# Stationary operands of the three-pass matmuls moved to 64 bytes behind the moving ones (modulo 512 bytes)

## The reference, cut to what matters

```
h = tok(x)                       # embedding + 4 layers; layer: x += ssm(ln(x)); x += gelu(ln(x) @ w1 + b1) @ w2 + b2
h = h + attn(layernorm(h))       # 16 heads of 16, Gaussian scores exp(-gamma * dist), masked, @ Wo
h = h + ffn(layernorm(h))        # 2 layers: shifted tokens, qkv (8 heads of 64), rotary, windowed softmax, @ wo,
                                 #           then gated MLP: a * gelu(g), width 682, @ w2
ssm(x) = scan(x @ B) @ C + x @ D # h[t] = sigmoid(a) * h[t-1] + u[t]
```

## Time and profile before

| | |
|---|---|
| three runs, us | 1294.94, 1297.45, 1292.15; median 1294.94 |
| span of the profiled execution, us | 1293.8 |
| median of the runs less that span, us | 1.1 |
| busy TensorE matmul, weight load | 94%, 80% |
| busy VectorE, ScalarE, GpSimd | 76%, 67%, 48% |
| granted TensorE clock, mean | 0.987 of full |

### The profile page before, as it was taken

One profiled execution on the slowest core, in us unless ns is written; L12 is line 12 of the kernel. 1 busy time (PEld: TensorE's weight loads), 2 busy tenths in 40 slices (PEclk: granted clock), 3 DMA queues, 4 the chain that ended last, 5 costly groups with the idle time before them and its releaser, 6 DMA issues.

```text
span 1293.8 us, 26097 instructions
## 1 busy us (share of the span) xinstructions
PE 1218.6 (94%) x8899; PEld 1035.8 (80%) x8899; DVE 988.7 (76%) x2624; ACT 860.9 (67%) x1989; POOL 618.5 (48%) x678
## 2 busy tenths in 40 slices
PE   5899999999999999799978899999999999999997
PEld 4699988988898989567756567888888887888796
DVE  5766676666667776799878988888888888888743
ACT  2455765676566556589964668777777777777754
POOL 6423341351145233455434568556556657655542
PEclk9999999999999999899989999999999999999999
DMA  7400010000000000310010002000100000000000
GB/s 170 112 1 15 2 65 0 14 32 32 0 8 1 1 1 1 75 49 18 18 53 17 1 5 93 6 5 6 49 4 3 21 6 13 22 22 22 22 17 26
DMA packets 39615, 33.25 MB, mean 26 GB/s; under 512 B 16774, under 2 KB 36178, under 8 KB 39506
## 3 DMA queue, kind: packets, MB, share of 16 engines
q1 hardware_dynamic: 38610, 29.74, 7.6%
q0 software_dynamic: 768, 2.10, 0.9%
q10 hardware_dynamic: 128, 0.04, 0.0%
HBM read 25.84 MB, written 4.19 MB: 23 GB/s over the span
## 4 chain that ended last, share of the span: by engine, by line
PE 45%; DVE 6%; ACT 3%; POOL 3%; issue 3%; DVEq 0%; ACTq 0%; POOLq 0%
PE w_ps_p L1887 3%; PE w_ring L1947 3%; PE w_ring L1948 3%; PE w_ring L1949 3%; PE w_ring L1846 3%; PE w_ring L1848 3%; PE w_ring L1847 3%; PE w_ps_a L1905 2%; PE a_ps L911 2%; PE w_ring L1959 2%; PE w_ps_d L1880 2%; PE w_ps_d L1877 2%; PE w_ring L1864 2%; PE w_ring L1960 2%; PE w_ring L1963 1%
## 5 line engine op out<-in xcount | busy, mean ns | idle before, releaser
L383 ACT ACTIVATE t_gf<-t_ps_f,t_fb_cur 128x512 f32<-128x512 f32 x128 | 87.9, 687 | 170.2 <-PE t_ps_f L289 167.0
L302 PE MATMUL t_ps_o<-t_w_hi,t_g_hi 128*128 128x256 f32 x512 | 146.1, 285 | 3.2 <-DVE t_g_lo L533 3.2
L533 DVE TENSOR_TENSOR t_g_lo<-t_gf,t_g_hi 128x512 fp32r<-128x512 f32 x128 | 94.4, 739 | 71.3 <-ACT t_g_hi L385 70.4
L304 PE MATMUL t_ps_o<-t_w_hi,t_g_lo 128*128 128x256 f32 x512 | 144.8, 283 | 0.0
L303 PE MATMUL t_ps_o<-t_w_lo,t_g_hi 128*128 128x256 f32 x512 | 144.7, 283 | 0.0
L686 POOL TENSOR_TENSOR t_rs<-t_ve,t_neghalf 128x4 f32<-128x4 f32 x32 | 37.9, 1185 | 168.0 <-DVE t_ve L494 166.6
L1947 PE MATMUL w_ring<-w_nh,w_w_hi 128*128 128x256 f32 x352 | 103.8, 295 | 3.3 <-DVE X L2546 1.7
L287 PE MATMUL t_ps_f<-t_nh,t_w_hi 128*128 128x512 f32 x256 | 103.0, 402 | 1.8 <-DVE t_nl L509 0.8
L302 PEld LDWEIGHTS t_ps_o<-t_w_hi,t_g_hi 128*128 128x128 f32 x512 | 97.7, 191 | 7.8 <-issue 4.4
L2717 POOL TENSOR_TENSOR w_m<-w_m 128x512 f32<-128x512 f32 x64 | 84.2, 1316 | 37.5 <-DVE w_m L2437 37.2
L288 PE MATMUL t_ps_f<-t_nh,t_w_lo 128*128 128x512 f32 x256 | 101.3, 396 | 0.0
(11 more groups left out here) (317 smaller groups left out, 4259.5 us busy)
## 6 DMA issues: line engine op xcount, KB each, us to landing
t_raw<-in_L_tok_w SPq DMA_DIRECT2D x8, 1024.0 KB, 5.2
out<-X SPq DMA_DIRECT2D x14, 256.0 KB, 2.2
raw<-in_L_ffn_wqkv SPq DMA_DIRECT2D x2, 1536.0 KB, 6.7
raw<-in_L_ffn_w SPq DMA_DIRECT2D x4, 640.0 KB, 5.0
w_raw_o<-out SPq DMA_DIRECT2D x8, 256.0 KB, 2.7
w_xs<-X SPq DMA_DIRECT2D x14, 127.0 KB
w_raw<-in_L_ffn_w SPq DMA_DIRECT2D x2, 640.0 KB
t_raw_d<-in_L_tok_D SPq DMA_DIRECT2D x4, 256.0 KB, 2.9
```

What stands on the lines that cost most here:

```text
L302: pe.matmul(out, g_hi[:, j % 4, tok], w2_hi[:, j, :], start=(j == 0 and t % 2 == 0), stop=False, skip_group_check=True)
L304: mm = pe.matmul(out, g_lo[:, j % 4, tok], w2_hi[:, j, :], start=False, stop=(j == FC - 1 and t % 2 == 1), skip_group_check=True)
L383: act.activation(gf[:, j % 2, :], ps_f[:, j % 2, :], ACT.Gelu, bias=fb_cur[:, j:j + 1]).then_inc(pf_free, 1)
L533: dve.tensor_tensor(g_lo[:, j % 4, :], gf[:, j % 2, :], g_hi[:, j % 4, :].bitcast(F32), ALU.subtract).then_inc(g_split, 1)
```

## The change

Empty buffers (`apart1`, `apart2`) are put in, and small ones are moved, so that in every three-pass matmul the stationary operand begins 64 bytes behind the moving one modulo 512 bytes. No instruction is added, removed or moved; only addresses change.

```
 tower:
+        sb("apart1", [P, 16])
         nf = [sb(f"nf{k}", [P, DC, GTOK]) for k in (1, 2)]
-        nh = [sb(f"nh{k}", [P, DC, GTOK], F32R) for k in (1, 2)]
-        nl = [sb(f"nl{k}", [P, DC, GTOK], F32R) for k in (1, 2)]
+        nh1, nl1 = (sb(x, [P, DC, GTOK], F32R) for x in ("nh1", "nl1"))
         hs = sb("hs", [P, GTOK])
...
         g_hi = sb("g_hi", [P, 4, GTOK], F32R)
         g_lo = sb("g_lo", [P, 4, GTOK], F32R)
+        sb("apart2", [P, 96])
+        nh2, nl2 = (sb(x, [P, DC, GTOK], F32R) for x in ("nh2", "nl2"))
+        nh, nl = [nh1, nh2], [nl1, nl2]
 attention:
         xn = [sb(f"xn{k}", [P, ST, D]) for k in range(2)]
+        sb("apart1", [P, 24])
         nh = sb("nh", [P, DC, STOK], F32R)
...
         sq = [sb(f"sq{t}", [P, 2 * D]) for t in range(ST)]
+        sb("apart2", [P, 64])
         ot_hi = sb("ot_hi", [P, HO, STOK], F32R)
 window_opening:
-    x0_ve = sb("x0_ve", [P, GT])
-    x0_rs = sb("x0_rs", [P, GT])
     xs = sb("xs", [P, 2, ST, P])
     ah = sb("ah", [P, DC, STOK], F32R)
     al = sb("al", [P, DC, STOK], F32R)
+    x0_ve = sb("x0_ve", [P, GT])
+    x0_rs = sb("x0_rs", [P, GT])
 window:
         nmr = sb("nmr", [P, ST])
+        mx = sb("mx", [P, 2 * H, 2])
         xn = sb("xn", [P, ST, D])
         nh = sb("nh", [P, DC, STOK], F32R)
...
         pt = sb("pt", [P, PTS, SC])
-        mx = sb("mx", [P, 2 * H, 2])
         rsum = sb("rsum", [P, SLOTS, 2])
```

## The result

The changed kernel takes 1287.28 us (median of 6 runs, 1283.3 to 1289.59) against 1294.4 (6 runs) before: 0.9933, interval 0.9914 to 0.9951, about 7 us less. 1276 was forecast and 1263 to 1290 given as the range. The time lies in the range, and the kernel is faster as forecast (the interval reaches the 0.5% that was named as the limit of a measurement); of the 18 us two fifths came.

A forecast was written before the change was run, and what follows sets the result against it. Matmul spacing was taken to bound tower and window, with VectorE and ScalarE equally full in attention. Gains of 25.1 us less 6.9 not kept left 18.2 us, giving 1276 us, range 1263 to 1290.

The forecast's parts named there:

- The bound: How closely matmuls follow each other sets the end in tower and window; in attention VectorE and ScalarE also do.
- (c): Tower `hidden`: 768 matmuls of 512 columns from 0 to +64, 6 ns gained each, 4.6 us.
- (e): Window phase `project`: 576 matmuls of 512 columns from 0 to +64, 6 ns gained each, 3.5 us.
- The bound from below (-6): Worst case for 512-column matmuls in tower and window: a loss of 6 ns each if +64 is no better than -32.
- (a): Tower `output`: 1536 matmuls of 256 columns from 0 to +64, 6 ns gained each, 9.2 us.
- (b): Tower `state_out`: 512 matmuls from 0 to +64, the same 6 ns gained each, 3.1 us.
- (d): Window phase `hidden_in`: 1056 matmuls from +192 to +64, 4 ns gained each, 4.2 us.
- (f): Attention: projections and `project_out` gain 1.5 us, of which a third, 0.5 us, reaches the end.
- (h): Gain not kept, lost to waits in tower and window phase: 3.8, 1.2 and 1.9 us, together 6.9.
- given back: Rival: chains over VectorE and ScalarE in tower and window keep perhaps a third, 8 us, 1287; chance 0.12.
- slower: Rival: 512-column matmuls in tower and window lose 25 ns each at +64, 17 us slower, 1312; chance 0.05.
- L302 stays at 283: Sign of failure: the tower `output` matmul at this line keeps a length of 283 instead of falling near 277.

The follow-up runs named there:

- hid_320: Kernel before with window-phase `hidden_in` at +320 and `project` at +192 bytes; one run took 1293.18 us beside a median of 1295.21.
- cols512: Kernel before with only the 512-column matmuls, tower `hidden` and window-phase `project`, moved to +64; 1297.14 us, ratio 1.0011.
- window_only: Kernel before with only the window phase's part of the change; 1292.55 us, ratio 0.9982.
- after_again: The changed kernel measured once more against the kernel before, for comparison on the same chip; 1286.19 us, ratio 0.9917.

## Why the prediction was wrong

**The bound** was right: what a matmul lost in spacing arrived in the time, and each phase's part added up. In the traces the tower, from the first start of `output` to its last, took 470.2 us before and 464.6 after; the window phase, from the first `hidden_in` to the last `hidden_out`, 502.2 and 498.8.

**The operands' offset as the cause** was right, and it is now shown and not only argued: in the window phase `hidden_in` went to 277 (+64, +320), 280 (+192, -64), 282 (+32, +128) and 283 (+256) as addresses moved and no instruction did. In `hid_320` its offset and `project`'s are the only ones of three-pass matmuls that changed (the buffers from `xn` to `pt` moved along). The rule of the Trainium skill ("TensorE: Matmul & The Clock Gate", Part 2) that a load takes nothing from the running matmul does not agree with this: 113.9 ns against 119.8 at `project_out`, same line and clock and the same instructions around it; the measurement decides. What in the chip makes load and matmul delay each other is not shown.

**Steps (c) and (e) failed.** They carried the 6 ns over to 512 columns, on the ground that the three matmuls have one form. From 0 to +64 the 512-column matmuls lost, averaged over the three passes, 2.0 ns by the lengths in `hidden` and 3.3 in `project`: 768 x 2 = 1.5 us and 576 x 3.3 = 1.9 us lost (1.4 ns each by the starts), where 4.6 and 3.5 were counted as gain. That is 11.5 us of the forecast's sum. The bound from below (-6) held; the value taken was wrong, and `cols512` shows it by itself: 1.0011. No offset that was tried made 512 columns more than a nanosecond quicker than 0 (the best is `project` at +192, 230.6 for 231.2).

**Steps (a) and (b): right mechanism, mis-sized.** 4 ns (3 at the first of each three) instead of 6 at `output`: 5.6 us for 9.2; 5 instead of 6 at `state_out`: 2.6 for 3.1. The 113.5 ns were read from a row at the quicker of two spacings; in the changed kernel about half of the `output` matmuls and three in ten of `state_out` take the longer one, near 118. Rows 5 held no sign of it, though L1960's 279 beside L1916's 277 at the same +64 was one.

**Step (d)** measured 3 ns by the lengths, 3.6 by the starts, for the 4 taken: 3.2 to 3.8 us for 4.2. **Step (f)** can't be told from noise: from the last `output` start of the tower to attention's last `project_out` start the traces have 160.3 us before, 158.8 after and 158.4 in `window_only`, which leaves attention as it was.

**Step (h)** was right in kind: the load waits of L233 and L274 grew, by 1.3 us together (0.05 us each time and not 0.1 to 0.2), where 3.8 were reckoned with a gain that the `hidden` blocks did not have. The tower's matmul waits of rows 3 went from 3.3 to 3.5 us for the 1.2 that were taken off, and in the window phase matmuls cover 395.5 of the same 400 us instead of 396.2, for the 1.9.

Put together by lengths: 5.6 + 2.6 - 1.5 + 3.2 - 1.9 + 0.5 (f, as forecast) - 1.3 = 7.2 us, against 7.1 between the medians. That they agree so closely is luck: by the starts the same sum is 9.4, and `after_again` measured 9.0. Of the 11 us that were missing, (c) and (e) account for 11.5 and (a), (b), (d) for 5.1, while (h) had taken some 5 us too much off. The rival "given back" names 8 us less, near the measured time, but is not what happened: waits took 1.3 us. The rival "slower" had the right step, 512 columns, with the wrong size: 2 to 3 ns and not 25. Two slips on the way change nothing: 1276.7 rounds to 1277, and the sign of failure "L302 stays at 283" names a line that had 285 (it fell to 282).

What stays open: why 512 columns don't gain, and what puts a row of 256 columns at 113 or at 118 ns. The load behind the transposes, the transition from `hidden` and the sign of the offset were tried and don't decide it by themselves. One difference stands in the traces, though no run tests whether it matters: a weight load takes 188 to 191 ns, longer than the 113 to 120 between matmuls of 256 columns and shorter than the 231 between those of 512.

## What to carry to other kernels

A gain per instruction that was read from one shape is for that shape: before it is multiplied by the count of another, look for a row of that shape, or weigh the whole of it as uncertain. Where two lines of one form differ by a few nanoseconds for no reason in the program, compare the residues of their operands' addresses; here 64 bytes were worth 3 to 5 ns on each of 3100 matmuls of 256 columns. Read a spacing over many rows, not over the one nearest: here rows of equal matmuls ran at 113 or at 118 ns.

## What was not expected of the hardware

For matmuls of 256 columns, offsets equal modulo 256 bytes gave equal spacings in the three pairs tried: 0 (`output`) and +256 119.5 to 119.8 ns, then for `hidden_in` +64 and +320 114, +192 and -64 117.6; +128, as far from 0 as can be in that period, gave 118.6, no better than +32 with 118.3. At 0 and +256 the weight load too was longer, 191 ns for 188. Matmuls of 512 columns stood 230 to 234 ns apart at 0, +32, +64, +128, +192, +256 and -64. And rows of equal matmuls with equal addresses ran at 113 or 118 ns from start to start, mostly one rhythm for a whole row of 12 to 36 matmuls.
